# A routed mixture of experts on one core: segments of 16, 10 and 6 tiles in place of 12, 12 and 8

## The reference

```
scores = sigmoid(xt @ gate_w.T);  idx = top_k(scores + gate_b, 4)
w = scores[idx] / sum(scores[idx]) * 2.5
y = sum over e of comb[:, e] * ((silu(xt @ Wg_e.T) * (xt @ Wu_e.T)) @ w2_e.T) + shared expert
x = x + s * silu(y)
```

## Time and profile before

| | |
|---|---|
| median of 3 runs | 560.62 us (559.27 to 569.72) |
| profiled execution | 564.42 us, span 562.4 us |
| busy in the span | PE 382.3 us (68%), VectorE 306.3 (54%), ScalarE 283.8 (50%), GpSimd 263.4 (47%) |
| DMA | 127.06 MB, mean 226 GB/s |
| granted TensorE clock, mean | 0.863 |

### The profile page before, as it was taken

The page is one execution under the profiler, slowest core; times in us unless marked ns, Lnnn a source line. Parts: engine busy times, 40 slices in busy tenths (PEclk is TensorE's granted clock), DMA queues, the critical chain, the costliest instruction groups (busy, mean ns, idle before and its releaser), DMA issues.

```text
span 562.4 us, 11496 instructions
## 1 busy us (share of the span) xinstructions
PE 382.3 (68%) x3631; PEld 302.1 (54%) x3631; DVE 306.3 (54%) x901; ACT 283.8 (50%) x531; POOL 263.4 (47%) x280
## 2 busy tenths in 40 slices
PE   0535457797985788697768989999954876775110
PEld 0423235465884677575556767778843765662000
DVE  4768556467750345632543588887611644383454
ACT  1571546677751455564555767777733654361000
POOL 2007757650017355565664656561065445503773
PEclk9999758889996699998997999999985988885555
DMA  7987839953765578668776899998664776534454
GB/s 248 386 269 242 292 114 327 341 172 123 247 224 195 173 241 292 215 194 267 243 240 201 265 303 267 346 301 254 209 190 143 222 242 205 174 121 140 140 147 124
DMA packets 106553, 127.06 MB, mean 226 GB/s; under 512 B 10241, under 2 KB 95874, under 8 KB 106498
## 3 DMA queue, kind: packets, MB, share of 16 engines
q1 hardware_dynamic: 92528, 92.17, 51.0%
q0 software_dynamic: 12288, 33.57, 18.8%
q10 hardware_dynamic: 1682, 0.59, 0.4%
HBM read 59.71 MB, written 66.58 MB: 225 GB/s over the span
## 4 chain that ended last, share of the span: by engine, by line
PE 30%; another core or an unknown queue 12%; issue 11%; DVE 11%; ACT 6%; POOL 5%; DMA 1%; ACTq 0%; POOLq 0%; DVEq 0%
PE bank L712 11%; PE bank L735 7%; POOL xn_parts L521 5%; PE bank L540 5%; PE bank L725 3%; DVE xn_parts L1295 3%; ACT xn_f L1515 2%; DVE xn_f L1244 2%; DVE sh_h L1250 1%; DVE sh_silu L1258 1%; ACT xn_f L1523 1%; PE bank L759 1%; DVE mix_sb L1272 1%; PE bank L764 1%
## 5 line engine op out<-in xcount | busy, mean ns | idle before, releaser
L499 POOL DMA_INDIRECT x_slots<-xn_parts,slot_u x128 | 130.6, 1021 | 159.7 <-DVE slot_e L993 45.3
L521 POOL DMA_INDIRECT xn_parts<-y_slots,slot_u x128 | 125.7, 982 | 131.3 <-DMA y_slots<-y_ring 48.9
L712 PE MATMUL bank<-w_all,xn_f 128*128 x1038 | 139.4, 285 | 14.1 <-issue 8.8
L1244 DVE SCALAR_TENSOR_TENSOR xn_f<-bank,xn_f 128x256 f32<-128x256 f32 x88 | 36.9, 420 | 167.3 <-ACT xn_f L1523 116.2
L712 PEld LDWEIGHTS bank<-w_all,xn_f 128*128 128x128 f16 x1038 | 101.8, 103 | 37.0 <-issue 22.4
L1515 ACT ACTIVATE xn_f<-bank 128x1024 f16<-128x1024 f16 x88 | 88.5, 1006 | 33.3 <-remote 20.4
L1539 ACT ACTIVATE y_ring<-bank 128x512 f32<-128x512 f32 x88 | 51.9, 590 | 79.2 <-remote 40.0
L735 PE MATMUL bank<-w_all,sh_silu 128*128 x519 | 79.0, 291 | 18.0 <-issue 9.0
L735 PEld LDWEIGHTS bank<-w_all,sh_silu 128*128 128x128 f16 x519 | 49.1, 105 | 28.5 <-issue 20.7
L540 PE MATMUL bank<-ident_h,w_stage 128*128 128x128 f16 x692 | 57.5, 228 | 4.1 <-issue 2.8
L1523 ACT ACTIVATE xn_f<-bank 128x256 f32<-128x256 f32 x88 | 33.4, 380 | 42.0 <-remote 22.5
(11 more groups left out here) (168 smaller groups left out, 469.7 us busy)
## 6 DMA issues: line engine op xcount, KB each, us to landing
w_stage<-x_slots SPq DMA_DIRECT2D x85, 256.0 KB
y_slots<-y_ring SPq DMA_DIRECT2D x85, 256.0 KB
x_ring<-in_x SPq DMA_DIRECT2D x32, 256.0 KB
x_slots<-zero_h SPq DMA_DIRECT2D x1, 8064.0 KB, 31.8
x_slots<-zero_h SPq DMA_DIRECT2D x7, 1024.0 KB
x_slots<-zero_h SPq DMA_DIRECT2D x7, 768.0 KB
w_stage<-in_w13t SPq DMA_DIRECT2D x17, 256.0 KB
x_ring<-in_x SPq DMA_DIRECT2D x8, 512.0 KB, 7.6
```

Of the source, the lines that this page charges most:

```text
L499: eng.indirect_dma_start(out=x_slots[s], out_offset=bass.IndirectOffsetOnAxis(ap=slot_u[:, n * TOPK + k:n * TOPK + k + 1], axis=0), in_=xn ...
L521: eng.indirect_dma_start(out=fin_y[:, r, j, k, :], out_offset=None, in_=y_slots[s], in_offset=bass.IndirectOffsetOnAxis(ap=slot_u[:, n * T ...
L712: mm = eng.matmul(gu[:, j * 2 * F:(j + 1) * 2 * F], xg_T[:, n % 2, ((j * 2 + px) * KD + k) * P:((j * 2 + px) * KD + k + 1) * P], w_all[:, ...
L1244: eng.scalar_tensor_tensor(out=h_sb[:, n % 2, 0:nb, :], in0=gv[:, 0:nb, F:2 * F], scalar=DESCALE, in1=silu_sb[:, n % 2, 0:nb, :], op0=ALU. ...
```

## The change

Segment 0 gets 16 tiles, segment 1 ten, segment 2 six. That gives 79, 55 and 39 blocks, 40 + 28 + 20 = 88 pairs. The routing groups become seven (4, 4, 4, 4 | 8, 2 | 6 tiles). Four batches are routed before the loop, in a new order on all engines; x batches 4 and 5 are loaded earlier, and the zero fill of segment 0 goes in two DMAs. The scatters of segment 0 are paced by other counts: tiles 1 to 3 by the steps of batch 0, tiles 4 to 15 by `gate_pre >= n - 2`. The pacing by pairs has new numbers for scatters, gathers and units. The last unit is done one tile at a time, with its gathers in the order tile, choice.

```diff
-SEG_TILES = (12, 12, 8)
-GROUP_TILES = (8, 4, 8, 4, 8)
+SEG_TILES = (16, 10, 6)
+GROUP_TILES = (4, 4, 4, 4, 8, 2, 6)
...
-    SCATTER_PAIR = (0, 7, 25)
-    SCATTER_PAIRS = (0, 18, 12)
+    SCATTER_PAIR = (0, 11, 31)
+    SCATTER_PAIRS = (0, 20, 12)
-    GATE_LEAD = 3
+    GATE_LEAD = 2
...
-        UNIT_PAIR = (41, 45, 49, 53, 57, 61, 71, 75, 78, 82, 85)
-        GATHER_PAIR = (37, 41, 45, 49, 53, 57, 67, 70, 73, 77, 80, 83)
+        UNIT_PAIR = (49, 53, 56, 60, 63, 67, 70, 74, 78, 81, 84)
+        GATHER_PAIR = (46, 49, 53, 56, 60, 63, 67, 70, 74, 77, 80, 83, 86)
...  SyncE
             for b in range(X_RING):
                 load_x(b)
+            load_weights(0)
+            eng.wait_ge(zeroed, 1)
+            fill(0, 0, 2)
+            load_x(X_RING)
+            load_x(X_RING + 1)
+            fill(0, 1, 2)
             eng.wait_ge(zeroed, 5)
-            fill(0)
...  GpSimd
+            def beside_gates(n):
+                if n == 1:
+                    eng.wait_ge(sh_silu_done, 1)
+                elif n == 2:
+                    eng.wait_ge(sh_hidden, 1)
+                elif n == 3:
+                    eng.wait_ge(sh_lo, 1)
+                elif n > 3:
+                    eng.wait_ge(gate_pre, n - GATE_LEAD)
...
-                    if s == 0 and n > GATE_LEAD:
-                        eng.wait_ge(gate_pre, n - GATE_LEAD)
+                    if s == 0:
+                        beside_gates(n)
...  TensorE, before the loop over batches
             x_transpose(0)
+            x_transpose_part(1, 0)
...
-            x_transpose(1)
+            x_transpose_part(1, 1)
             route_batch(1)
-            bias_products()
+            x_transpose(2)
+            x_transpose_part(3, 0)
+            route_batch(2)
+            x_transpose_part(3, 1)
+            route_batch(3)
             eng.wait_ge(before_set, 1)
-            x_transpose(2)
-            route_batch(2)
-            rank(0)
-            rank(1)
+            for g in SEG_GROUPS[0]:
+                rank(g)
             eng.wait_ge(tri_set, 2)
             block_counts(0)
             block_starts(0)
+            bias_products()
             blocks_ended(0)
             for b in range(NB):
-                if 0 < b < NB - 2:
-                    x_transpose(b + 2)
+                if 0 < b < NB - 3:
+                    x_transpose(b + 3)
...  VectorE, before the loop
-            norm_ratio(0)
+            norm_stats(2)
             state_weights()
-            gate_bias_rows()
-            norm_stats(2)
             norm_stats(3)
             x_low(0)
+            norm_scale(1)
             x_transposed(0)
             x_low(1)
+            choose_scores(0)
             x_transposed(1)
...
             choose(1)
+            choose(2)
+            choose(3)
+            gate_bias_rows()
+            weights_low(0)
             block_counts(0)
             block_starts(0)
...
-            weights_low(0)
...  VectorE, in the loop
-                if b + 3 < NB:
-                    x_low(b + 3)
+                if b == 0:
+                    norm_scale(2)
...
+                if b + 4 < NB:
+                    x_low(b + 4)
...  the last unit on VectorE
-            multiply(NU - 1)
-            add_x(NU - 1)
+            for k in range(TOPK):
+                combine_last(0, k)
+            multiply(LAST - 1)
+            add_x(LAST - 1)
+            for k in range(TOPK - 1):
+                combine_last(1, k)
+            multiply_last(0)
+            add_x_last(0)
+            combine_last(1, TOPK - 1)
+            multiply_last(1)
+            add_x_last(1)
```

More of the change, by code:

```diff
@@ L250, in recurrent_gated_moe @@
         filled = [sem(f"filled{s}") for s in range(NSEG)]
-        x_slotted = [sem(f"x_slotted{b}") for b in range(NB)]
+        x_slotted = {(s, b): sem(f"x_slotted{s}_{b}") for s in range(NSEG) for b in SEG_BATCHES[s]}
         xb_in = [sem(f"x_block_in{i}") for i in range(XB_RING)]
@@ L333, in in_tail, with tile_order @@
             return c >= len(UNIT_PAIR) or SLOTS * UNIT_PAIR[c] + offset >= SLOTS * (NPAIR + 2)
+        def tile_order(c):
+            if c < NU - 1:
+                return [(k, j) for k in range(TOPK) for j in range(FT)]
+            return [(k, j) for j in range(FT) for k in range(TOPK)]
         def xb_at(n):
@@ L459, in _ @@
                     store_out(c - 1)
-            store_out(NU - 1)
-            eng.wait_ge(stored, 16 * NU)
+            for j in range(FT):
+                n = (NU - 1) * FT + j
+                eng.wait_ge(summed, NU + j)
+                eng.dma_start(o_view[:, n, :], mix_sb[:, n, :]).then_inc(stored, 16)
+            eng.wait_ge(stored, 16 * (NU - 1 + FT))
         @block.gpsimd
@@ L510, in gather_y @@
                 if c == 0:
-                    for b in range(NB):
-                        eng.wait_ge(x_slotted[b], 16 * TOPK * BT)
+                    for seg, b in x_slotted:
+                        eng.wait_ge(x_slotted[seg, b], 16 * TOPK * tiles_in(seg, b))
                 if c >= FIN_RING:
                     eng.wait_ge(product, c - FIN_RING + 1)
[L515 to L524, removed]
+                for k, j in tile_order(c):
+                    n = c * FT + j
+                    if c < len(GATHER_PAIR):
+                        i = k * FT + j
+                        eng.wait_ge(pair_t, GATHER_PAIR[c] + i * GATHER_PAIRS[s] // (TOPK * FT))
+                    eng.indirect_dma_start(
+                        out=fin_y[:, r, j, k, :], out_offset=None, in_=y_slots[s],
+                        in_offset=bass.IndirectOffsetOnAxis(ap=slot_u[:, n * TOPK + k:n * TOPK + k + 1], axis=0))\
+                        .then_inc(y_last if c == NU - 1 and j == 0 else y_in[r][k], 16)
             for s in range(NSEG):
@@ L541, in transposed, with x_transpose_part @@
                 t.then_inc(signal, 1)
-            def x_transpose(b):
[L544 to L548, removed]
-                    transposed(part, lambda j: xn_parts[:, s, j % BT, part, (j // BT) * P:(j // BT + 1) * P], 2 * BT, x_t)
+            def x_transpose_part(b, part):
+                s, made, taken = b % XN_RING, (x_hi, x_lo)[part], (xT_hi, xT_lo)[part]
+                eng.wait_ge(made, b + 1)
+                if b:
+                    eng.wait_ge(taken, b)
+                transposed(part, lambda j: xn_parts[:, s, j % BT, part, (j // BT) * P:(j // BT + 1) * P], 2 * BT, x_t)
+            def x_transpose(b):
+                x_transpose_part(b, 0)
+                x_transpose_part(b, 1)
             def route_batch(b):
@@ L1329, in beside @@
                         block_starts(s)
-                for g, first in ((2, 18), (3, 20), (4, 42)):
+                for g, first in ((4, 18), (5, 20), (6, 42)):
                     if slot == first:
@@ L1376, in _ @@
                 beside(SLOTS * n + 2)
-            for c in range(len(UNIT_PAIR) - 1, NU):
+            for c in range(len(UNIT_PAIR) - 1, NU - 1):
                 for k in range(TOPK - 1):
@@ L1588, in _ @@
                     pair_y_out(n - 2)
-            for c in range(len(UNIT_PAIR) - 1, NU):
+            for c in range(len(UNIT_PAIR) - 1, NU - 1):
                 if in_tail(c, SILU):
                     silu(c)
+            for j in range(FT):
+                s = fin_sum[:, (NU - 1) % FIN_RING, j, :]
+                eng.wait_ge(combined, TOPK * (FT * (NU - 1) + j + 1))
+                eng.activation(s, s, ACT.Silu, scale=1.0 / WS).then_inc(silu_done, 1)
 def kernel(**inputs):
```

106 lines of the change are left out of this document (70 added, 36 removed).

## The result

In the first measurement, the condition that the forecast was made for, the changed kernel takes 532.18 us (median of 4 runs, 528.93 to 533.63), the kernel before 564.39 (559.27 to 569.72): a ratio of 0.9496, with 0.942 to 0.9573 as its interval, 5% faster. The profiled executions took 532.27 and 564.42 us, 32.15 us apart; the sum of the prediction says 20.9. On other chips of the same kind the kernel before took 467.5 to 468.6 us, and on the one of them that ran the unedited change too, it is 2% slower (ratio 1.0202, 1.0156 to 1.0248). Both results are real, and most of what follows is about what tells them apart.

The account below looks back on a forecast made before the run. It blamed GpSimd's indirect DMAs: bursts stalling the core in pairs 9, 10, 69, 70, plus head and tail. Terms summed to -20.9 us: 543.5 profiled, 539.7 median; own range 532 to 549, whole range 520 to 564.

Parts of the forecast that it names:

- rival (a): Better: scatter stage at the gathers' price, gather stage with pauses enough, head at +4; about 522 with half of each; chance 0.15.
- scatter stage: Pairs 11 to 42: 64 scatters, two per pair, at 4.0 us a pair, 128 against 111.8: +16 us (+1 to +31).
- Head: Before pair 0: 16 more scatters delay the first loads, +9 us (0 to +13).
- pacing bound: Lower bound in the head: last tile waits for the 13th count of gates, giving 138.0, +6, or about +4 with earlier waiting.
- The rest of the head order is taken at nothing: Head: other reordering costs 0; one more VectorE group against two norm steps moved out, 3 us more if uncovered.
- Pairs 9 and 10: Segment 1's scatters begin at pair 11, so no burst: two pairs at 3.95 in place of 22.1, -14.2 us.
- Free pairs: Pairs 43 to 45 without scatters or gathers in place of 60 to 68: 8.2 against 24.7, -16.5 us.
- Gather stage: Pairs 46 to 86, 12 units: 169 us against 174.1, -5 us, as the catching-up burst goes but groups of three pairs cost more.
- no pair over 8 us: Sign in the pair phase: if the forecast holds, no single pair takes more than 8 us.
- rival (d): Gather stage: GpSimd never empty, so the 14.6 us stall returns; three times make 583.5, slower; chance 0.07.
- Tail, drain, last unit: After the last pair: 24 gathers in place of 32, -10.1 us; drain delayed, +1; last unit one tile at a time, -1.1.
- rival (c): Slow stretches not made by bursts: +14.2 and +14.6 come back wherever GpSimd begins a segment, 568.5; chance 0.07.

Follow-up runs that it names:

- skipped scatters: Changed kernel without the 16 scatters of tiles 12 to 15, whose routed experts then add nothing: 460.84 us, ratio 0.9852 to the kernel before.
- unpaced head: Changed kernel with segment 0's scatters freed of their waits on batch steps: 471.29 us (ratio 1.0067 to the kernel before), repeated at 471.92 us (1.0069).
- prompt condition: Runs on chips where the unedited kernel before takes 467.5 to 468.6 us; the unedited changed kernel took 477.37 us there, ratio 1.0202.
- late condition: Runs where the unedited kernel before takes 564 to 566 us, as in the first measurement; the changed kernel took 532.18 us there, ratio 0.9496.
- second: Group of runs with both kernels unedited, the changed kernel without 16 scatters, and it with segments of 12, 14, 6 tiles; kernel before 467.51 us.
- fourth group: Repeats of the changed kernel with 2.7 scatters per pair (477.61 us) and with head scatters freed of batch waits (471.92 us); kernel before 468.63 us.

## Why the prediction came out as it did

The forecast was 539.7 with a range of 520 to 564; the measured 532.2 lies in it, at the edge of the forecast's own 532 to 549, and faster was right. What the prediction calls rival (a) came true in one term, the scatter stage. Its terms, forecast and measured, in the condition in which it was made:

- **Head: +9, measured +14.9.** This term failed upward, outside its own bounds (0 to +13). The working by GpSimd's rate came near: 143.6 for the last scatter, measured 145.95, and +12 in all. Going down from there towards the pacing bound was the error. There are pauses of 14.6 us in all before scatters, for gates of later batches, where the kernel before has 7.2. The prediction called the head GpSimd's in the kernel before as well; there the last scatter started 16.6 us before the first load, so the batches hid part of the 16 new scatters: the last one moved by 30.7 us, pair 0 by 14.9. The skipped scatters (pair 0 16.1 us earlier) show that GpSimd decides in the kernel after, and the unpaced head (6.2 to 6.3 us less, by the ratios) what the pacing costs in the prompt condition. "The rest of the head order is taken at nothing" was wrong where signals are prompt: 6.5 to 7.3 us with 12 tiles. What it is where they are late is not measured.
- **Pairs 0 to 8: nothing, measured +1.6.** The granted clock was 0.92, after 15.6 us at 0.50 with TensorE almost idle, and 1.00 in the kernel before. Without the 16 scatters, and so without that wait, it was 1.00 and the 1.7 us were gone (27.34 for 29.05, prompt).
- **Pairs 9 and 10: -14.2, measured -13.0.** The mechanism is shown: put the burst back, and 17.8 us return in the same two pairs.
- **Scatter stage: +16, measured -1.8** (109.99 against 111.8 us). This is the term that was mis-sized. I took the middle, 4.0 us, between the gathers' 3.53 and the 4.47 of the dense scatters. It was 3.44, below the lower end: at two for each pair almost nothing of the price is left (0.2 us for each pair, above).
- **Free pairs: -16.5, measured -16.7** (8.01 against 24.7).
- **Gather stage: -5, measured -8.9** (165.2 against 174.1). The burst of catching up at pair 70 is gone. The groups of three were not free: pairs 69, 74 and 83 take 7.6, 7.6 and 9.2 us, against the sign "no pair over 8 us", and waits marked "remote" of up to 4.7 us are there. The last 17 pairs of the kernel after, late and then prompt (all engines), are 21.8 us apart: that much of rival (d)'s mechanism is in the result. In the kernel before the same pairs, 412.06 to 497.56, are 85.5 us late and 50.7 prompt, 34.8 apart, so it was smaller than what it replaced.

```profile
400.55:473.67 73.12, 57.62 (x533) 46.41 (x533) 39.91 (x102) 39.07 (x75) 40.98 (x42) 0.88 0.71 215
```

```profile
371.60:422.92 51.32, 49.75 (x536) 43.17 (x537) 39.57 (x102) 39.75 (x74) 39.42 (x40) 1.00 0.97 314
```

- **Tail, drain, last unit: -10.2, measured -8.3.** The drain is 1.3 us longer (17.64 for 16.3) where 1 was taken. The 24 last gathers take 1.35 us each (32.39 / 24) in place of 1.27, so they are 8.2 us shorter and not 10.1. The end behind them is 1.5 shorter for 1.1 forecast.

These sum to -32.2, and the 11.3 us by which the sum of 20.9 is off are made up so: scatter stage -17.8, gather stage -3.9, free pairs -0.2, against head +5.9, tail +1.9, pairs 0 to 8 +1.6, pairs 9 and 10 +1.2. The forecast was as near as it was by luck in part: the two large errors, scatter stage and head, have opposite signs. It was luck too that the result was taken in the late condition; in the other one the change is 2% slower, and of the rivals only (c) comes near that.

**The rule against which the rows were set.** The prediction set the rows against the Trainium skill, "DMA: Bandwidth & Descriptors", section "SWDGE vs HWDGE vs iDMA": software and hardware DMAs are in different queues, and each DMA engine takes turns. By it a burst costs its share of bandwidth and no more, and the change gives nothing back in the stalls. That last step is the prediction's own. Where signals are prompt it is what was measured: the burst cost nothing and the change made the kernel 2% slower. In the late condition it does not hold: 17.8 us for 16 DMAs moved into two pairs, which are lost in the counts of TensorE and not in the DMA engines' turns. What the prediction got wrong about it is its rank: rival (c), "The slow stretches are not made by bursts", had a chance of 0.07 as if it were a question of fact about the chip, and it turned out to depend on which chip, or when.

**Still open:** what makes TensorE's counts late. The kernel, the DMA instruction's own length and the fill's landing (31.8 us late, 32.0 prompt, for 8064 KB) are the same. One thing goes with it in all 14 traces: the late ones hold only 1466 to 1497 records of counts set by engines and 4081 to 4624 set by DMAs, the prompt ones 1938 to 1974 and 8723 to 8996, for about the same program. So it isn't excluded that recording the trace takes part in the delay. The late runs and the prompt ones were never on one and the same chip as far as the runs tell. One chip was prompt in the second and in the fourth group, 25 minutes apart, and another was late between them, which speaks for the chip and against the hour, but does not settle it.

## What to carry to other kernels

Price a stall by what makes it and ask whether it is always there: a trace of one execution is a trace of one chip's condition, and the stalls here whose releaser the profile calls "remote" vanished in the other. The page shows the condition at once: in the chain that ended last, "another core or an unknown queue" holds 6 to 12% in the four late traces and does not occur in the ten prompt ones.

Pacing GpSimd's DMAs so that the count never runs ahead of their data avoids a burst, because what is owed is issued in a row. Where signals are late it took 12 and 18 us off the burst at pair 9. Only the kernel after kept the gain as a whole (550.26 with the burst, 532.18 without, in different groups); in the kernel before another burst took its place, and 0.6% was left. Where signals are prompt it gained nothing: the kernel after is the same with the burst, and the kernel before was 1.3% slower without it. Work moved ahead of the first pair to make it possible is paid in both conditions: +14.9 us late and +23.4 prompt here, with 16 more indirect DMAs in the head.

## What was not expected of the hardware

- The same kernel takes 564 to 566 us in one condition and 467.5 to 468.6 in the other, a fifth apart, each steady within some 2%. With no indirect DMA beside them pairs take the same: pairs 0 to 8 are 27.56 and 27.47 us.
- While GpSimd issues indirect DMAs in a row, a finished product was seen 12.4 us late in the late condition and 0.04 us late in the prompt one, with the DMA instructions 0.96 us long and 0.30 apart in both. Only counts that TensorE sets are late.
- The price is far from linear: two scatters for each pair cost 0.2 us, 2.7 cost 1.0, 18 in a row 17.8 in all.
- Gathers in groups of four pairs, 28 in 14 pairs, cost nothing even in the late condition: pairs 46 to 59 of the kernel before take 47.24 us late and 47.32 prompt (there with 33 gathers). With 33 gathers in the same 14 pairs, 2.4 for each, they are not free: the kernel after takes 53.13 us late and 45.12 prompt. The lines, in this order:

```profile
336.08:383.32 47.24, 43.95 (x467) 37.60 (x466) 40.56 (x98) 35.38 (x67) 28.81 (x28) 1.00 0.95 303
```

```profile
278.60:325.92 47.32, 44.12 (x461) 37.31 (x461) 38.58 (x94) 35.74 (x66) 32.67 (x33) 0.98 0.94 305
```

```profile
308.47:361.60 53.13, 45.59 (x457) 37.37 (x456) 35.91 (x87) 34.91 (x66) 33.20 (x33) 0.97 0.89 272
```

```profile
295.15:340.27 45.12, 42.68 (x455) 36.40 (x454) 35.53 (x87) 35.23 (x67) 32.62 (x33) 1.00 0.99 328
```
